# New tables in an embedding and interaction network: which tiles are split, by whom, and when gathers are issued

## What is computed

```python
e = jnp.stack([tbl_0[ids[:, 0]], ..., tbl_38[ids[:, 38]]], axis=1)
x0 = xk = e
for idx, (W, b) in enumerate(params):
    z = jnp.einsum('bhd,bkd,hks->bsd', x0, xk, W) + b[None, :, None]
    z = jax.nn.relu(z)
    if idx != n_layers - 1:
        half = z.shape[1] // 2
        xk = z[:, :half, :]
        direct.append(z[:, half:, :])
    else:
        direct.append(z)
logit = jnp.sum(jnp.concatenate(direct, axis=1), axis=-1)
...
h = jnp.concatenate([z, dense_ctx], axis=1)
h = jnp.maximum(h @ W_top1 + b_top1, 0.0)
h = jnp.maximum(h @ W_top2 + b_top2, 0.0)
y = h @ W_top3
```

## Time and profile before

| | us |
|---|---|
| median of 3 runs (1243.71 to 1244.59) | 1243.73 |
| the profiled run | 1244.94 |
| its span in the trace | 1243.1 |
| PE, DVE, ACT, POOL busy | 1179.9, 1061.9, 580.7, 1002.6 |
| granted TensorE clock, mean | 0.999 |

### The profile page before, as it was taken

The page is one execution under the profiler, slowest core; times in us unless marked ns, Lnnn a source line. Parts: engine busy times, 40 slices in busy tenths (PEclk is TensorE's granted clock), DMA queues, the critical chain, the costliest instruction groups (busy, mean ns, idle before and its releaser), DMA issues.

```text
span 1243.1 us, 14868 instructions
## 1 busy us (share of the span) xinstructions
PE 1179.9 (95%) x3856; PEld 726.5 (58%) x3856; DVE 1061.9 (85%) x927; ACT 580.7 (47%) x563; POOL 1002.6 (81%) x629
## 2 busy tenths in 40 slices
PE   0289999999999999999999999999999999999999
PEld 0155666656565665656566565656656565666665
DVE  2278998989899898989889898998989898998984
ACT  1145444444545444454544445454444545444545
POOL 6678897998889899888989888888988889765651
PEclk9999999999999999999999999999999999999999
DMA  4785726365472626556262745637274563627000
GB/s 125 242 256 191 223 63 218 125 182 201 157 226 60 218 108 206 177 172 211 84 204 97 225 159 172 211 102 215 79 233 140 172 211 123 212 72 231 9 1 1
DMA packets 110269, 196.21 MB, mean 158 GB/s; under 512 B 52975, under 2 KB 64334, under 8 KB 110249
## 3 DMA queue, kind: packets, MB, share of 16 engines
q1 hardware_dynamic: 100009, 193.33, 47.2%
q0 software_dynamic: 10240, 2.64, 2.0%
HBM read 193.36 MB, written 12.78 MB: 166 GB/s over the span
## 4 chain that ended last, share of the span: by engine, by line
PE 69%; POOL 13%; DVE 8%; issue 6%; ACT 2%; DMA 2%; POOLq 0%; SPq 0%; DVEq 0%; ACTq 0%
PE acc L845 67%; POOL lo L464 7%; POOL emb L454 6%; DVE prod L706 3%; DVE lo L719 2%; ACT hi L556 2%; DVE acc L706 1%; DVE hi L716 1%; DMA x_tiles<-x_rows 0%; DMA x_rows<-x_rows 0%; DVE xk L706 0%; PE acc L925 0%; POOLq L163 0%; DMA x_rows<-emb 0%; ACT xk L522 0%
## 5 line engine op out<-in xcount | busy, mean ns | idle before, releaser
L706 DVE TENSOR_TENSOR prod<-x_tiles,xk 128x1024 f32<-128x1024 f32 (+2 forms) x643 | 757.5, 1215 | 123.9 <-PE acc L845 83.4
L464 POOL TENSOR_TENSOR lo<-prod,hi 128x1024 fp32r<-128x1024 f32 (+1 forms) x288 | 690.5, 2400 | 141.1 <-ACT hi L556 136.4
L845 PE MATMUL acc<-prod,wfull 128*128 128x512 f32 (+2 forms) x1408 | 660.6, 593 | 0.0
L556 ACT ACTIVATE hi<-prod 128x1024 fp32r<-128x1024 f32 (+1 forms) x291 | 308.4, 1060 | 406.3 <-DVE prod L706 322.4
L845 PE MATMUL acc<-hi,whi 128*128 128x512 f32 (+1 forms) x800 | 353.0, 441 | 57.7 <-ACT hi L556 57.6
L845 PEld LDWEIGHTS acc<-prod,wfull 128*128 128x128 f32 (+2 forms) x1408 | 266.8, 189 | 205.7 <-issue 177.4
L454 POOL DMA_INDIRECT emb<-table,block_idx x320 | 308.6, 964 | 69.3 <-issue 63.9
L845 PE MATMUL acc<-lo,whi 128*128 128x512 f32 (+1 forms) x736 | 316.1, 517 | 2.4 <-POOL lo L464 1.2
L845 PE MATMUL acc<-hi,wlo 128*128 128x512 f32 (+1 forms) x800 | 316.1, 395 | 0.0
L845 PEld LDWEIGHTS acc<-hi,whi 128*128 128x128 f32 (+1 forms) x800 | 150.9, 189 | 112.4 <-issue 72.2
L845 PEld LDWEIGHTS acc<-lo,whi 128*128 128x128 f32 (+1 forms) x736 | 138.3, 190 | 133.2 <-issue 104.0
(11 more groups left out here) (72 smaller groups left out, 163.4 us busy)
## 6 DMA issues: line engine op xcount, KB each, us to landing
x_tiles<-x_rows SPq DMA_DIRECT2D x304, 512.0 KB, 5.1
x_rows<-x_rows SPq DMA_DIRECT2D x16, 624.0 KB
x_tiles<-x_rows SPq DMA_DIRECT2D x32, 256.0 KB, 5.6
x_stack<-x_rows SPq DMA_DIRECT2D x48, 156.0 KB
emb<-table,block_idx POOLq DMA_INDIRECT x320, 3.8
x_rows<-emb SPq DMA_DIRECT2D x16, 152.0 KB, 3.3
x_tiles<-w SPq DMA_DIRECT2D x1, 768.0 KB, 6.1
x_tiles<-w SPq DMA_DIRECT2D x1, 704.0 KB, 8.6
```

Source lines behind the costliest of these rows:

```text
L464: nc.gpsimd.tensor_tensor(lo[0:r, product_slot(j), :], prod[0:r, product_slot(j), :], hi[0:r, part_slot(j), :].bitcast(f32), ALU.subtract) ...
L556: nc.scalar.activation(hi[0:r, part_slot(j), :], held(n, parity, j)[0:r, :], ACT.Copy).then_inc(hi_ready, 1)
L706: nc.vector.tensor_tensor(held(n, parity, j)[0:r, :], in0, in1, ALU.mult).then_inc(product_ready, 1)
L845: mm = nc.tensor.matmul(z[:, c], w[0:r], part[0:r, c], start=first and i == 0, stop=last and i == len(weights) - 1)
```

## The change

Three tables and two counts are new, and with them the places of waits.

- `KINDS`: layer 0 has four G and three F (before two and five); layer 1 has seven G, four D, one H and eight F (before eight, three, one, eight); layer 2 has seven G, four D, one H and eight F (before eight, two, one, nine). A block has 19 F, 18 G, 8 D and 2 H, where it had 22, 18, 5 and 2. The order within the layers is another one as well.
- `PRODS` is 7 and `PARTS` is 5.
- ScalarE, before it writes a hi slot that a G tile held, waits for that tile's hi pass (new semaphore `hi_used`) and for GpSimd's subtraction, and no longer for its lo pass on TensorE.
- The gathers stand in runs of one, two, three and five at chosen places. In the prologue sixteen instead of twelve stand ahead of the first subtraction, and the other four behind all four.
- `WRITE_AFTER` is 12.
- The second last tile of layers 1 and 2 is a D now, and its subtraction stands one product behind, not two.
- The code around `SQUARE` keeps the place of the first tile's weights general; with this table it is still 0.

```diff
-KINDS = ["GFFGFFF", "GFDGF" * 2 + "GFHGF" + "GFDGF", "GFFGF" + "GFFGD" + "GFHGF" + "GFDGF"]
+KINDS = ["GGFGFGF", "GDFGGDFFDFGGHFGGFFDF", "FFFGFFDGGDFGHGGDGFDF"]
...
-PRODS, PARTS = 6, 4
+PRODS, PARTS = 7, 5
...
-            WRITE_AFTER = 9
+            WRITE_AFTER = REST - 1
...
-            gather(1, 0, 12)
-
-            def layer(n, l, m=None, parity=0, gathers=(0, 0)):
-
-                at, tiles = (L0, L1, L2)[l], [t for t, k in enumerate(KINDS[l]) if k == "G"]
-                start, stop = gathers
-                between = max(1, len(tiles) - (4 if l == 2 else 0))
-                for i, t in enumerate(tiles):
-                    subtract(n, at + t)
-                    if m is not None and i < between:
-                        gather(parity, start + i * (stop - start) // between,
-                               start + (i + 1) * (stop - start) // between)
-
-
-
-            GATHERS = {1: (0, 8), 0: (8, 12), 2: (12, PAIRS)}
-            layer(PROLOGUE, 0, 1, 1, (12, PAIRS))
+            gather(1, 0, 16)
+
+            def layer(n, l, m=None, parity=0, gathers=()):
+
+                tiles = [j for j in range((L0, L1, L2)[l], (L0, L1, L2)[l] + len(KINDS[l])) if KIND[j] == "G"]
+                assert m is None or sum(gathers) == 0 or len(gathers) == len(tiles)
+                start = 0 if l == 1 else sum(GATHERS[1]) if l == 0 else PAIRS - sum(GATHERS[2])
+                for i, j in enumerate(tiles):
+                    subtract(n, j)
+                    if m is not None:
+                        gather(parity, start, start + gathers[i])
+                        start += gathers[i]
+
+            GATHERS = [[0, 0, 0, 5], [1, 0, 3, 0, 2, 0, 3], [1, 1, 1, 0, 0, 1, 2]]
+            assert sum(map(sum, GATHERS)) == PAIRS
+            for j in [j for j in range(L0, L2) if KIND[j] == "G"]:
+                subtract(PROLOGUE, j)
+            gather(1, 16, PAIRS)
...
-                            act.wait_ge(tile_used, reached(n, parts_before(n, j), "FDGH"))
+                            held_by = parts_before(n, j)
+                            if KIND[held_by] == "G":
+
+                                act.wait_ge(hi_used, reached(n, held_by, "G"))
+                                act.wait_ge(lo_ready_g, reached(n, held_by, "G"))
+                            else:
+                                act.wait_ge(tile_used, reached(n, held_by, "FDGH"))
...
-            DELAY = 2
+            def wait_of(j):
+
+                return 1 if j in (L0 - 2, STEP - 2) else 2
...
-                            multiply(j, [whi[:, w, :], wlo[:, w, :]], hi[:, part_slot(j), :], j == start, False)
+                            mm = multiply(j, [whi[:, w, :], wlo[:, w, :]], hi[:, part_slot(j), :], j == start, False)
+                            if KIND[j] == "G":
+                                mm.then_inc(hi_used, 1)
```

More of the change, by code:

```diff
@@ L71 @@
 FULLS = [[t for t, k in enumerate(ks) if k == "F"] for ks in KINDS]
+SQUARE = (SPLITS[0] + FULLS[0]).index(0)
 SPLIT_AT = [0, len(SPLITS[0]), len(SPLITS[0]) + len(SPLITS[1])]
@@ L248, in build @@
         lo_ready_d = sem("lo_ready_d")
+        hi_used = sem("hi_used")
         lo_ready_g = sem("lo_ready_g")
@@ L311, in load_weights @@
                 sp.dma_start(w0f_stage[0:LAST0, len(FULLS[0]) - 1, :], w0[0:LAST0, T0 - 1, :]).then_inc(w0_loaded, 16)
-                sp.dma_start(w0t_stage[0:ROWS0, 1:T0 - 1, :], w0t[:, 1:T0 - 1, :]).then_inc(w0_loaded, 16)
+                if SQUARE:
+                    sp.dma_start(w0t_stage[0:ROWS0, 0:SQUARE, :], w0t[:, 0:SQUARE, :]).then_inc(w0_loaded, 16)
+                sp.dma_start(w0t_stage[0:ROWS0, SQUARE + 1:T0 - 1, :], w0t[:, SQUARE + 1:T0 - 1, :]).then_inc(w0_loaded, 16)
                 sp.dma_start(w0t_stage[0:LAST0, T0 - 1, :], w0t[0:LAST0, T0 - 1, :]).then_inc(w0_loaded, 16)
                 sp.wait_ge(w0_cleared, 1)
-                sp.dma_start(w0t_stage[FIELDS:ROWS0, 0, :], w0t[FIELDS:ROWS0, 0, :]).then_inc(w0_loaded, 16)
+                sp.dma_start(w0t_stage[FIELDS:ROWS0, SQUARE, :], w0t[FIELDS:ROWS0, SQUARE, :]).then_inc(w0_loaded, 16)
                 for l, b in enumerate((b0, b1, b2)):
@@ L670, in _ @@
         def _(dve):
-            nc.vector.memset(w0t_stage[:, 0, :], 0.0).then_inc(w0_cleared, 1)
+            nc.vector.memset(w0t_stage[:, SQUARE, :], 0.0).then_inc(w0_cleared, 1)
             nc.vector.memset(direct2[:, :], 0.0).then_inc(direct2_cleared, 1)
             dve.wait_ge(direct2_cleared, 1)
-            dve.wait_ge(w0_loaded, 6 * 16)
+            dve.wait_ge(w0_loaded, (6 + (SQUARE > 0)) * 16)
             n, f = len(SPLITS[0]), len(FULLS[0])
@@ L750, in tiles @@
                     product(n, parity, j)
-                    if j - DELAY >= start and KIND[j - DELAY] in "DH":
-                        subtract(n, parity, j - DELAY)
+                    for i in (j - 2, j - 1):
+                        if i >= start and KIND[i] in "DH" and i + wait_of(i) == j:
+                            subtract(n, parity, i)
                     if l == 1 and t == T1 // 2 and past_end(n, 1):
@@ L758, in tiles @@
                         sum_direct01(n)
-                for j in range(stop - DELAY, stop):
-                    if KIND[j] in "DH":
-                        subtract(n, parity, j)
+                for i in range(stop - 2, stop):
+                    if KIND[i] in "DH" and i + wait_of(i) >= stop:
+                        subtract(n, parity, i)
             def clear_top(n):
```

## The result

The changed kernel takes 1228.56 us in the median of 4 runs (1227.85 to 1228.98), the kernel before 1244.16 beside it (4 runs, 1243.71 to 1244.87). The ratio is 0.987, with an interval of 0.986 to 0.989: faster by 15.6 us, where 19.6 were forecast. The span of the profiled run went from 1243.1 to 1227.1.

The account below looks back on a forecast made before the run. TensorE was taken as the bound, busy 71.71 of a 71.84 us block. Fifteen blocks at -1.32 (-19.8), prologue -0.5, last layer 2 -0.34 and tail +1.0 made -19.6: from 1243.73 to 1224.1, forecast 1224, range 1221 to 1232.

Parts of the forecast that it names:

- rival 1: GpSimd sets the pace at one or two places, above all layer 0's end: 0.3 to 0.8 a block, 1227 to 1235; chance 0.20.
- The swaps: Three F tiles a block become D, each 1.38 instead of 1.72 us on TensorE: 1.02 us less, all on the path.
- Rival 4: The swaps bring TensorE nothing, because something unseen sits between its passes: about 1244; chance 0.04.
- The stall that goes: In layer 2 TensorE's lo pass waits 0.40 us for GpSimd in each old block; this wait was to go.
- New small stalls: Whatever replaces the old stall in a block, bounded by nothing and 0.40, taken as 0.10 us.
- the wait costs nothing by itself: VectorE's wait, about 1.8 us, at layer 2's first D for layer 0's accumulator; TensorE wants that hi 4 us later.
- rival 2: VectorE becomes the bound, its own 68.6 and 1.8 of accumulator wait leaving nothing: 1231 to 1239; chance 0.10.
- The walk of GpSimd's queue at the end of layer 0: GpSimd's four layer 0 subtractions followed against TensorE's wishes; the last lo 0.2 us early, the block's tightest place.
- Slots and waits: Seven product slots, five hi slots and earlier hi freeing: 0 on the path; the second wait also 0.
- Rival 3: The later rows chain makes VectorE stand at its first layer 0 tile every block; 9 us late gives 1254; chance 0.04.
- Prologue: Layer 0 run once with two Fs less, sixteen gathers ahead of GpSimd's first subtraction: -0.5, between 0 and -0.7.
- Last layer 2 and tail: Last block: layer 2 saves 0.34; VectorE and GpSimd holding each other up over SBUF costs +1.0, between -0.5 and +3.

Follow-up runs that it names:

- e11_one_less: The kernel of e2_dshift with the D tile at place 7 of layer 2 turned back to F; 1227.26 us, block 70.65.
- e2_dshift: The changed kernel with layer 2's first two D tiles one place later, the second subtracted one product behind; 1222.71 us, block 70.30.
- e4_prods6: The changed kernel with six product slots instead of seven; 1232.09 us, block 70.89.
- e6_lo_frees: The changed kernel with the early freeing of hi slots undone, so ScalarE waits for the lo pass as before; 1226.29 us, block 70.52.
- e12_write9: The changed kernel with the write of the gathered rows back after the tenth tile of layer 2; 1226.84 us, block 70.65.
- e8_slots_only: The kernel before with seven product slots and five hi slots, nothing else; 1243.18 us, ratio 0.999.
- e7_spread: The changed kernel with the gathers spread as evenly as before; 1337.15 us, ratio 1.074.

## Why the prediction was right, and where it was not

The time, 1228.56, lies 4.6 us over the forecast of 1224: inside the range (1221 to 1232) and on the side that was called likely, but above the forecast's own 1221 to 1227, where rival 1 had its times. By its steps:

- **What bounds the kernel**: right. TensorE is busy for the whole block in both, and the time moved with what TensorE does and waits for.
- **The swaps, -1.02 a block**: right, and measured alone, 0.34 for one of them (e11_one_less). Rival 4 is out.
- **The stall that goes, -0.40**: right in kind and too small. The block with the fewest stalls is 70.30 (e2_dshift), which is what the tiles alone add up to by the prediction's prices, 19 x 1.72 + 26 x 1.38 + 2 x 0.90 = 70.4. So the kernel before lost at least 71.87 - 1.02 - 70.30 = 0.55 in the block; the prediction took the one pause it saw.
- **New small stalls, +0.10**: this term was too small, at 70.66 - 70.30 = 0.36 (0.26 in layer 1, 0.11 in layer 0). The sum is -1.02 - 0.55 + 0.36 = -1.21 a block. The two errors partly cancel.
- **Why that term was too small**: the step was "the wait costs nothing by itself". The size of the wait was right (2.05 us, forecast about 1.8; own work 68.65, forecast 68.6), and the D tile itself was in time. But the prediction looked only at that tile's hi, and the bill comes some forty microseconds later, where a product is late that has no cover of its own. The sentence that the wait used up VectorE's cover said this, and it was then counted as nothing. Of the rivals it is a mixture: one place was that of rival 1 (end of layer 0, GpSimd's lo) and so was the size (0.36, of 0.3 to 0.8), but the cause was that of rival 2 (VectorE), which had been given 0.10.
- **The walk of GpSimd's queue at the end of layer 0**: it gave the fourth lo 8.3 us after TensorE's start, 0.2 ahead of the wish at 8.5. Measured 8.92. It started its count at the third hi, behind the emptying; in the trace GpSimd works through all four without a pause, 4 x 2.37, and what counts is when the first hi comes. "The walk shows cover everywhere" was also too much for layer 1, where the pair at 652.30 began 1.85 us after GpSimd was free.
- **Slots and waits, 0**: off by the seventh product slot, 0.23 us a block (e4_prods6), and by the early freeing in the other direction. The "second wait in front of each such hi" was counted as 0; it costs 0.14 us a hi, and e6_lo_frees, without it, has a block 0.14 shorter. The two pieces partly cancel. The fifth hi slot was not tried alone.
- **The rows chain, 0**: right (e12_write9 has the same block). The write stood where it was expected, and VectorE waited for no transfer. Rival 3 is out.
- **The place of the gathers**: right that it pays by place, and more than was thought: 7 to 9 us a block between the table as changed and the even spread.
- **Prologue, -0.5**: failed. "It loses little" left out that the pause for the first lo can come while TensorE is at its starting pace. The first layer 0 came at +1.48 and, in a second execution, at -0.24; with twelve gathers at -1.33. The +1.48 are a start 1.86 earlier (51.02 against 52.88, which varies between executions as well), 2.19 more to layer 1, and 1.15 more in layer 1 of block 0, at half pace.
- **Last layer 2 and tail, -0.34 + 1.0**: with the fifteenth block's -1.32, which lies in the same stretch, -0.66 was forecast behind the last layer 0's start, and -0.51 was measured. Part of this is luck. The slots, counted as 0, take 1.9 from this stretch in the kernel before (e8_slots_only); if that holds here too, the tables cost some 1.4 where they were to save 0.66. VectorE was held up twice, as said, by 1.04 and 1.07; the meeting that cost 2.2 of 3.42 went. GpSimd was held up four times (3.3 to 3.5 us instead of 2.4), and TensorE waited 0.68 for it.
- **What a meeting costs**: the prediction read 1.1 to 1.5 us against a rule of the Trainium skill ("SBUF — State Buffer", "Who interferes with whom") and found the rule too high. The rule is that the shared ports are an exclusive lock, and the trace agrees with it to a few hundredths: the second instruction ends 1.08 us (VectorE) or 2.25 us (GpSimd) behind the end of the first, whenever it came. 2.4 is only the most that VectorE can lose, if both come at once.

Together: 14 blocks at -1.21, +1.48 and -0.51 are -16.0 in the span; forecast were -19.6. Of the 3.6 that lack, 14 x 0.11 = 1.5 lie in the blocks. The other 2.1 are nearly all at the start: -0.5 was forecast, for layer 1 of block 0 has as many F tiles as before, and +1.48 came. The start itself varies by 1.7 between two executions of one kernel.

## What to carry to other kernels

An engine whose own work and unavoidable waits add up to the whole period has no cover, even if every single wait is in time for its own tile: add them up around the loop, and look for the late product far behind the wait. Before a tile is given to the engine with the least room, move the point where it must wait, by one place if that is enough (here 5.3 to 5.9 us for five letters of a table and one distance). One more wait in front of an instruction isn't free, even if it is met by then, where other engines stand for that instruction. Count a pause of TensorE at more than its length if the clock can fall behind it or has not yet risen, and place transfers that an engine issues where nobody waits for what stands behind them.

## What the runs showed of the hardware

- Short pauses can lower the clock. In e7_spread TensorE stood idle 1.86 us ahead of a lo pass at the end of layer 0, was busy all the time afterwards, and the granted clock was 0.50 for the next 6.8 us. It fell in eight of fourteen blocks, though a pause of 1.8 to 1.9 us stands there in all of them. In the changed kernel the clock of the block was 1.00, with stalls of 0.1 to 0.3 us.
- The slow start has no fixed length: full pace came 9.5 us after the first matmul in one execution of the changed kernel and 4.2 in another, and 3.2 to 9.5 over all traces. The first F took 3.62 and 1.88. The distance of the starts shows it; the window view prints 1.00 there, but these traces hold no clock record from before full pace begins. With it the first layer 0 came at 103.95 in one execution and at 102.23 in another.
- VectorE and GpSimd, each subtracting two operands that lie in SBUF, don't share: the later one begins its work when the earlier one has ended (1.08 and 2.25 us from that end to its own). With one operand in PSUM VectorE takes 1.22 us beside a working GpSimd.
- One more wait in front of an instruction of ScalarE delays its start by 0.14 us, even if it is met before the one that comes last (0.17 us behind the product instead of 0.03, in 140 places).
